# A mixture-of-experts stage on one Trainium2 core: routing scores in four column groups of TensorE, and two experts' weight splits moved to other places

## What is computed

```python
# layer 0, attention: even rows of each segment of 256 attend to each other, 16 heads of width 16, q = k = v
scores = jnp.einsum('bsqhd,bskhd->bshqk', qh, qh) * scale
attn = jax.nn.softmax(scores, axis=-1)
seg_out = jnp.einsum('bshqk,bskhd->bsqhd', attn, qh)
...
# layer 0, experts: E = 8, DIM = 256, FFN = 1024, x has 4096 rows
logits = x @ router_w + router_b
route = jax.nn.softmax(logits, axis=1)
max_prob = jnp.max(route, axis=1, keepdims=True)
max_ind = jnp.argmax(route, axis=1)
for e in range(num_experts):
    h = x @ w1[e]
    a, g = jnp.split(h, 2, axis=1)
    y = jax.nn.silu(a) * g @ w2[e]
    out = jnp.where((max_ind == e)[:, None], y, out)
out = out * max_prob
```

## Time and profile before

| quantity | value |
|---|---|
| runs, median (lowest, highest) | 1685.89 us (1683.33, 1692.66), 3 runs |
| the profiled execution, own time | 1684.51 us |
| its span, first to last instruction | 1682.8 us |
| mean granted TensorE clock | 0.937 of full speed |
| busy: PE, DVE, ACT, POOL | 1423.0, 941.7, 603.7, 668.2 us |

### The profile page before, as it was taken

One profiled execution on the slowest core, in us unless ns is written; L12 is line 12 of the kernel. 1 busy time (PEld: TensorE's weight loads), 2 busy tenths in 40 slices (PEclk: granted clock), 3 DMA queues, 4 the chain that ended last, 5 costly groups with the idle time before them and its releaser, 6 DMA issues. The chain is left out here.

```text
span 1682.8 us, 27329 instructions
## 1 busy us (share of the span) xinstructions
PE 1423.0 (85%) x8858; PEld 1216.5 (72%) x8859; DVE 941.7 (56%) x1802; ACT 603.7 (36%) x1015; POOL 668.2 (40%) x501
## 2 busy tenths in 40 slices
PE   6994546989989996499957999999999985999997
PEld 3442235878878885377756888888888874999997
DVE  4778441344444332377565776776776762555555
ACT  3443311222222332377532322322322322555553
POOL 6553344555555001511014555555555550531400
PEclk9996767999999998699978999999999997999999
DMA  4101332222120002600031253553543546554541
GB/s 147 54 25 58 118 127 76 84 86 93 68 100 19 16 13 76 206 1 1 1 100 51 63 140 110 150 137 112 150 134 115 150 132 230 188 191 167 192 143 44
DMA packets 109176, 171.15 MB, mean 102 GB/s; under 512 B 6112, under 2 KB 95072, under 8 KB 101696
## 3 DMA queue, kind: packets, MB, share of 16 engines
q1 hardware_dynamic: 100096, 156.00, 28.6%
q0 software_dynamic: 3408, 9.31, 1.9%
q10 hardware_dynamic: 5616, 5.11, 0.9%
HBM read 114.96 MB, written 55.44 MB: 101 GB/s over the span
## 5 line engine op out<-in xcount | busy, mean ns | idle before, releaser
L1448 PE MATMUL disp_psS<-disp_e,last_x 128*128 128x256 f32 x1024 | 240.4, 389 | 39.2 <-POOL disp_e L1538 20.5
L1448 PEld LDWEIGHTS disp_psS<-disp_e,last_x 128*128 128x128 f32 x1024 | 193.6, 194 | 70.9 <-POOL disp_e L1538 25.6
L1538 POOL TENSOR_TENSOR disp_e<-disp_e,disp_rs 128x1024 f32<-128x1024 f32 x64 | 152.4, 2380 | 119.9 <-DVE disp_rs L1567 119.9
L1567 DVE RECIPROCAL disp_rs<-disp_rs 128x256 f32<-128x256 f32 x64 | 112.2, 1753 | 135.4 <-POOL disp_rs L1536 135.4
L1498 ACT ACTIVATE disp_raw<-disp_psL 128x512 f32<-128x512 f32 x128 | 76.1, 595 | 290.2 <-DVE disp_top L1579 220.3
L1706 PE MATMUL comb_psO<-comb_yh,comb_eh 128*128 (+1 forms) x512 | 155.6, 304 | 14.1 <-DVE comb_el L1797 10.5
L1534 POOL TENSOR_TENSOR disp_s<-disp_e 128x512 f32<-128x512 f32 x64 | 81.6, 1275 | 203.5 <-ACT disp_e L1520 203.5
L1433 PE MATMUL disp_psL<-phi_hi,disp_xh 128*128 (+1 forms) x512 | 156.3, 305 | 5.4 <-DVE disp_e L1587 5.4
L1433 PE MATMUL disp_psL<-phi_lo,disp_xh 128*128 (+1 forms) x512 | 145.2, 284 | 0.0
L1433 PE MATMUL disp_psL<-phi_hi,disp_xl 128*128 (+1 forms) x512 | 145.0, 283 | 0.0
L1706 PE MATMUL comb_psO<-comb_yh,comb_el 128*128 (+1 forms) x512 | 144.7, 283 | 0.0
(11 more groups left out here) (256 smaller groups left out, 3537.6 us busy)
## 6 DMA issues: line engine op xcount, KB each, us to landing
logits<-disp_raw SPq DMA_DIRECT2D x64, 512.0 KB, 4.0
comb_e<-logits SPq DMA_DIRECT2D x32, 1024.0 KB, 4.9
w_raw<-in_w SPq DMA_DIRECT2D x8, 2048.0 KB
disp_wt<-in_w_slot SPq DMA_DIRECT2D x16, 1024.0 KB, 8.6
w_raw<-in_w SPq DMA_DIRECT2D x8, 1024.0 KB
disp_bt<-in_b_slot SPq DMA_DIRECT2D x8, 1024.0 KB, 11.3
slot_y<-disp_yb SPq DMA_DIRECT2D x64, 128.0 KB, 2.7
comb_y_in<-slot_y SPq DMA_DIRECT2D x4, 2048.0 KB, 10.3
```

The source lines that it names most:

```text
L1448: last = nc.tensor.matmul(psS[kd][:, b, :], x[:, b * TB + mc, kd * P:(kd + 1) * P], e[mc % 4][:, b, :], start=mc == 0 and b % 2 == 0, stop ...
L1538: nc.gpsimd.tensor_tensor(e[mc % 4][:], e[mc % 4][:], rs[mc % 2][:].unsqueeze(1).to_broadcast([P, B, BLK]), ALU.mult).then_inc(share_ready, 1)
L1567: v.reciprocal(rs[mc % 2][:], rs[mc % 2][:]).then_inc(rsum_ready, 1)
```

## The change

Four edits.

1. Router scores: the router's weights `rw` stand in 32 columns per chunk (`EW`), of which the last 24 are zero (POOL clears the buffer first, and SP's load waits for that). A group's four tiles are scored by eight products with 128 columns moving, tile `a` into output partitions 32a to 32a+31 of one 128x128 PSUM tile. ACT copies 128x128 in place of 8x512, and one transpose turns back four tiles' scores. DVE reads the 8 live columns of 32.
2. Expert 0's split leaves the routing block. ACT makes 1/16 of the high part per segment of the attention, after the copy of the next segment's rows (`high_slice`, 256 and 128 columns), and POOL 1/16 of the low part, two segments behind its masks (`low_slice`).
3. Expert 1's low part leaves the routing block: POOL makes it in the experts block, between the fourth and the fifth gather.
4. SP's load of expert 1 waits on `split` as before; the count is now reached by the attention's last slice.

```diff
--- before.py
+++ after.py
@@ -176,6 +176,7 @@
         out_raw, outT_ready, out_turned, rden_ready, heads_ready, fin, ones_set = (
             m.sem(s) for s in ("out_raw", "outT_ready", "out_turned", "rden_ready", "heads_ready", "fin", "ones_set"))
         even_loaded = [m.sem(f"even_loaded{i}") for i in range(2)]
+        w0_high = m.sem("w0_high")
         block = ctx.enter_context(nc.Block())
 
         def pair(i, k, lag):
@@ -235,11 +236,17 @@
                         xm[g][:], xT[q][:, half, :].unsqueeze(1).to_broadcast([P, UH, P]),
                         c["headmask"][:, part * UH:(part + 1) * UH].unsqueeze(2).to_broadcast([P, UH, P]),
                         ALU.mult).then_inc(xm_ready, 1)
+                    if g == UPS - 1:
+                        seg = i * 2 + q - 2
+                        if not isinstance(i, int) or seg >= 0:
+                            weights.low_slice(pool, seg, w0_high)
 
             fill_constants(nc, c, pool)
             masks(0)
             with pool.Fori(1, NSEG // 2) as i:
                 masks(i)
+            for seg in range(NSEG - 2, NSEG):
+                weights.low_slice(pool, seg, w0_high)
 
         @block.tensor
         def _(pe):
@@ -379,6 +386,9 @@
                 at = segment(i, k, -1)
                 if at is not None:
                     augment(*at, i + 1 + (k + 1) // 4)
+                at = segment(i, k, 3)
+                if at is not None:
+                    weights.high_slice(act, at[0], w0_high)
 
             keep_x(0, 0)
             act.wait_ge(ones_set, 4)
@@ -498,6 +508,7 @@
     m = Scope(nc, ctx, "route")
     XB = 3
     GT = 4
+    EW = P // GT
     with ctx:
         mean = m.sb("mean", [P, NT])
         rstd = m.sb("rstd", [P, NT])
@@ -505,8 +516,8 @@
         tmp = m.sb("tmp", [P, NT])
         magic = m.sb("magic", [P, NT], I32)
         xT = [m.sb(f"xT{i}", [P, KD, GT, P]) for i in range(2)]
-        logit_t = [m.sb(f"logit_t{i}", [NE, GT * P]) for i in range(2)]
-        rw = m.sb("rw", [P, KD, NE])
+        logit_t = [m.sb(f"logit_t{i}", [P, P]) for i in range(2)]
+        rw = m.sb("rw", [P, KD, EW])
         rb = m.sb("rb", [P, NE])
         logit = m.sb("logit", [P, NT, NE])
         best = m.sb("best", [P, NT])
@@ -530,11 +541,12 @@
         slots1 = m.sb("slots1", [P, NT, NCOL])
         ids = m.sb("ids", [P, NT, 2 * NCOL], BF16)
         psX = [m.ps(f"psX{i}", [P, 2, KD, P]) for i in range(XB)]
-        psL = [m.ps(f"psL{i}", [NE, GT * P]) for i in range(2)]
-        psR = m.ps("psR", [P, NT, NE])
+        psL = m.ps("psL", [P, P])
+        psR = m.ps("psR", [P, NT, EW])
         psAB = m.ps("psAB", [P, 2, NT, NE])
         psA, psB = psAB[:, 0], psAB[:, 1]
         psI = m.ps("psI", [P, 2 * NCOL])
+        rw_clear = m.sem("rw_clear")
         (w_loaded, chain, kept, turned, xT_ready, scored, scores_ready, routed, diff_ready, exp_ready,
          onehot_ready, counted, tables_ready, gathered, stored) = (m.sem(s) for s in (
              "w_loaded", "chain", "kept", "turned", "xT_ready", "scored", "scores_ready", "routed", "diff_ready",
@@ -543,7 +555,8 @@
 
         @block.sync
         def _(sp):
-            sp.dma_start(rw[:], router_w.rearrange("(k p) e -> p k e", p=P)).then_inc(w_loaded, 16)
+            sp.wait_ge(rw_clear, 1)
+            sp.dma_start(rw[:, :, 0:NE], router_w.rearrange("(k p) e -> p k e", p=P)).then_inc(w_loaded, 16)
             sp.dma_start(rb[:], router_b.partition_broadcast(P)).then_inc(w_loaded, 16)
             weights.load(sp, 1)
             for b in range(B):
@@ -554,8 +567,7 @@
 
         @block.gpsimd
         def _(pool):
-            weights.divide_low(pool, 0)
-            weights.divide_low(pool, 1)
+            nc.gpsimd.memset(rw[:], 0.0).then_inc(rw_clear, 1)
 
         @block.tensor
         def _(pe):
@@ -569,17 +581,17 @@
 
             def score(g):
                 wait(pe, xT_ready, g * 2 + 2)
-                wait(pe, scores_ready, g - 1)
+                wait(pe, scores_ready, g)
                 for k in range(KD):
-                    last = nc.tensor.matmul(psL[g % 2][:], rw[:, k, :], xT[g % 2][:, k].rearrange("p a t -> p (a t)"),
-                                            start=k == 0, stop=k == KD - 1)
+                    for a in range(GT):
+                        last = nc.tensor.matmul(psL[a * EW:(a + 1) * EW, :], rw[:, k, :], xT[g % 2][:, k, a, :],
+                                                start=k == 0, stop=k == KD - 1, skip_group_check=True)
                 last.then_inc(scored, 1)
 
             def turn_back(g):
                 wait(pe, scores_ready, g + 1)
-                for a in range(GT):
-                    last = nc.tensor.transpose(psR[:, g * GT + a, :], logit_t[g % 2][:, a * P:(a + 1) * P], c["ident"][0:NE, 0:NE])
-                last.then_inc(routed, 1)
+                nc.tensor.transpose(psR[:, g * GT:(g + 1) * GT, :].rearrange("p t e -> p (t e)"), logit_t[g % 2][:],
+                                    c["ident"][:]).then_inc(routed, 1)
 
             pe.wait_ge(w_loaded, 32)
 
@@ -605,12 +617,10 @@
 
         @block.scalar
         def _(act):
-            weights.divide_high(act, 0)
-
             def out(g):
                 act.wait_ge(scored, g + 1)
                 wait(act, routed, g - 1)
-                nc.scalar.activation(logit_t[g % 2][:], psL[g % 2][:], ACT.Copy).then_inc(scores_ready, 1)
+                nc.scalar.activation(logit_t[g % 2][:], psL[:], ACT.Copy).then_inc(scores_ready, 1)
 
             for i in range(NT // 2):
                 g = i // 2
@@ -642,7 +652,7 @@
                 v.tensor_scalar(x1[:, t, :], x1[:, t, :], mean[:, t:t + 1], rstd[:, t:t + 1], ALU.subtract, ALU.mult).then_inc(kept, 1)
             dve.wait_ge(w_loaded, 32)
             dve.wait_ge(routed, NT // GT)
-            link(v.tensor_tensor(logit[:], psR[:], rb[:].unsqueeze(1).to_broadcast([P, NT, NE]), ALU.add))
+            link(v.tensor_tensor(logit[:], psR[:, :, 0:NE], rb[:].unsqueeze(1).to_broadcast([P, NT, NE]), ALU.add))
 
             link(v.tensor_reduce(best[:], logit[:], X, ALU.max))
             bc = lambda ap: ap.unsqueeze(2).to_broadcast([P, NT, NE])
@@ -745,6 +755,24 @@
         sp.dma_start(self.raw1[:], self.w1_dram[e].rearrange("(k p) f -> p k f", p=P)).then_inc(self.loaded1, 16)
         sp.dma_start(self.raw2[:], self.w2_dram[e].rearrange("(k p) d -> p k d", p=P)).then_inc(self.loaded2, 16)
 
+    def high_slice(self, act, seg, ready):
+
+        for loaded, raw, hi, _ in self.parts():
+            act.wait_ge(loaded, 16)
+            n = KD * 2 * FF // NSEG if raw is self.raw1 else FK * D // NSEG
+            last = self.nc.scalar.activation(hi[:, 0, bass.ds(seg * n, n)], raw[:].rearrange("p k f -> p (k f)")[:, bass.ds(seg * n, n)], ACT.Copy)
+        last.then_inc(ready, 1)
+
+    def low_slice(self, pool, seg, ready):
+
+        pool.wait_ge(ready, seg + 1)
+        for _, raw, hi, lo in self.parts():
+            n = KD * 2 * FF // NSEG if raw is self.raw1 else FK * D // NSEG
+            last = self.nc.gpsimd.tensor_tensor(lo[:, 0, bass.ds(seg * n, n)], raw[:].rearrange("p k f -> p (k f)")[:, bass.ds(seg * n, n)],
+                                                hi[:, 0, bass.ds(seg * n, n)].bitcast(F32), ALU.subtract)
+        if isinstance(seg, int) and seg == NSEG - 1:
+            last.then_inc(self.split, 4)
+
     def parts(self):
         return ((self.loaded1, self.raw1, self.hi1, self.lo1), (self.loaded2, self.raw2, self.hi2, self.lo2))
 
@@ -757,7 +785,7 @@
     def divide_low(self, pool, e):
 
         for n, (_, raw, hi, lo) in enumerate(self.parts()):
-            pool.wait_ge(self.high, 2 * e + n + 1)
+            pool.wait_ge(self.high, 2 * (e - 1) + n + 1)
             self.nc.gpsimd.tensor_tensor(lo[:, e, :], raw[:].rearrange("p k f -> p (k f)"), hi[:, e, :].bitcast(F32),
                                          ALU.subtract).then_inc(self.split, 2)
 
@@ -836,6 +864,8 @@
                                              bass.IndirectOffsetOnAxis(route["token"][:, slot:slot + 1], 0)).then_inc(gathered[q], 16)
 
             for slot in range(SLOTS):
+                if slot == 4:
+                    w.divide_low(pool, 1)
                 gather(slot)
             nc.gpsimd.memset(w.zero[:], 0.0).then_inc(w.zeroed, 1)
             pool.wait_ge(w.zeroed, 1)
```

## The result

| group | kernel before, median (runs) | changed kernel, median (runs) | ratio, 95% interval |
|---|---|---|---|
| first pair | 1687.43 (4) | 1671.14 (4) | 0.9901 [0.9879, 0.9924] |
| 2 | 1650.56 (7) | 1617.82 (4) | 0.9819 [0.9781, 0.9857] |
| 3 | 1652.44 (7) | 1620.07 (4) | 0.9803 [0.9779, 0.9827] |
| 4 | 1653.81 (7) | 1618.61 (4) | 0.9798 [0.9764, 0.9833] |
| 5 | 1688.27 (9) | 1668.14 (2) | 0.9889 [0.9813, 0.9965] |

The forecast was 1649 and the range 1640 to 1664; the first pair gave 1671.14, so the change is faster, but by 16 us and not by 36. The kernel before has two levels, 1650 to 1654 in four of these groups and in group 1 (1650.00), and 1687 to 1688 in two, so kernels are compared only within a group.

The account below looks back on a forecast made before the run. The prediction had POOL's SBUF subtractions stalling DVE, and so PE, in routing, PE pacing the scores, and gathers delaying PE's reports in the experts: 1684.5 - 24.0 - 12.4 + 0.5 + 0 = 1648.6, forecast 1649, range 1640 to 1664.

Parts of the forecast that it names:

- Norm and scores: Routing: without POOL's subtraction and with narrow score products, DVE starts the logit sum at 165.4 instead of 189.44, saving 24.0 us.
- the extra 0.18: Scores on PE: two changes between full and narrow form per group, 0.09 us each, raising a group from 1.72 to 1.90.
- Counting: Routing: DVE's five additions take at most 2.3 us instead of 14.69, saving 12.4 us.
- Attention: Expert 0's split slices on ACT and POOL fit in gaps; cost taken 0.5 us for the block, bounds 0 and 18.
- Experts: Expert 1's low part between gathers makes the stream end 13.5 us later; cost taken 0, bounds -20 and +13.5.
- the hold: Experts: what PE reports reaches other engines late during POOL's gathers, at worst until 3.9 us behind the last.
- The rival with the longer hold: Experts: PE's reports stay late longer because the gather stream ends 13.5 us later; 1662.5 us, chance 0.12.
- a late report of PE: During a stream of POOL's gathers, what PE reports reaches the others late, at worst only when the stream is over.
- the forecast of that wait's end: Experts: ACT's longest wait should end 4 us behind the last gather, near 70 us from the first.
- The case "nobody is held": Experts: the gathers delay no engine, as the reason for the delay isn't known; 1629 us, chance 0.06.

Follow-up runs that it names:

- one gather more in front: Changed kernel with expert 1's low part behind five gathers instead of four: 1618.11 us, against 1617.82 for the changed kernel.
- the kernel with nine late gathers: Changed kernel with expert 1's low part behind five gathers and the last nine gathers behind expert 2's split: 1616.00 us; 1647.34 in group 5.
- Groups 4 and 5: Changed kernel with expert 1's low part back in the routing block: 1626.28 against 1618.61 us, then 1671.24 against 1668.14.
- The twelve pieces: Changed kernel with expert 1's low part as twelve instructions of 512 columns, still between the fourth and fifth gather: 1614.36 us, one run.
- the six pieces: Changed kernel with expert 1's low part in six pieces of 1024 columns, one behind every six gathers: 1629.44 us.
- the four gathers: Changed kernel with only the first four gathers, every slot's rows read from those four tiles in turn: 1622.02 us, one run.
- group 6: Changed kernel with ten gathers, expert 1's low part behind the fifth, then expert 2's split, then the other 29 gathers: 1638.28 us, against 1619.68 for the changed kernel.

## Why the prediction was wrong

- **Norm and scores** (24.0 saved): right, 23.0 by the rows (189.44 to 166.40). A group was to take 1.90 and took 1.70. The sum without the extra 0.18 was 1.72, and the 0.18 was counted twice: each change of form costs the 0.09 that was read in the attention, but the 1.02 and the 0.57 went from the start of one form to the start of the next and already held one such step each. In the narrow view of PE (the last transpose, the turning back, the first of the narrow products) two starts of one form are 0.11 apart, and the start of the new form is 0.21 behind the last of the old:

```profile
156.47 0.27 PE L579 MATMUL route_psX<-const_ident,first_x 128*128 128x128 f32 x1
156.58 0.27 PE L593 MATMUL route_psR<-const_ident,route_logit_t 128*128 128x128 f32 x1
156.79 0.32 PE L587 MATMUL route_psL<-route_xT,route_rw 128*32 128x128 f32 x4
```

The Trainium skill (TensorEngine Tiling (Array Packing), Tiling Modes, Key Properties) states that a change of the tiling mode drains TensorE; the 0.1 us more agrees with it. What six groups gave so, 1.1 us, was less than the 1.9 by which the first scores ended later than forecast (153.86, not 152.0); 1.55 of that is a later start of the norm (148.39 against 146.84), which is no cost of the change: two profiles of each kernel show both values (146.6 to 146.8, and 148.4).
- **Counting** (12.4 saved): right, 12.42 (14.69 to 2.27).
- **Attention** (0.5): POOL's slices took 1.14 where 1.13 was said and lay in its gap; masks still start every 7.6 to 7.7 us.
- **Experts** (0 taken, 17.8 lost): here it failed. The failed step is the sentence that the first 13.5 us "are now free of gathers, and PE gets one to two slots further before it is held". It gets no further. One result is out before the hold, as before: the first comes at 39.4 behind the first gather (33.1 in group 5), the second at 68.8 (69.0), and so 12.5 later than before, as the stream ends 12.1 later (64.5 against 52.4). In the meantime PE even falls back: it starts the last of the third slot's first products (L897) at 41.9 behind the first gather, and in the kernel before (L867) at 32.4.
- **What took the quiet time**: in part POOL's low part, which holds DVE's copy of the second slot's rows for 13.66 us, and PE waits 5.44 for it. The prediction had read this same lock in routing and priced it in the attention, and left it out where the 13.45 us had been moved to. In group 2, without the stretch, the lock costs 4.7 at the first result and one gather more in front takes that away (26.6). With the stretch it is argued, not shown by itself: the kernel with nine late gathers, whose copy is free, is a slot further (second result at 43.2, stream to 53.5; the kernel before 56.3, stream to 52.4), but the changed kernel with only the fifth gather moved wasn't run in a group with the stretch. The other 8 of the 13 us at the first result (39.4 against 31.2 in group 2) came with the stretch, with idle times of PE and ACT behind 220 put down to "issue" and "remote".
- First the row, then the rule: the copy stood for 13.66 us beside two POOL instructions of 13.40 together. The Trainium skill (SBUF — State Buffer, SBUF: two separate sides) states that a GpSimd instruction and a DVE one in a two-port mode or with two SBUF inputs shut each other out for a whole instruction; the trace agrees, and goes further, with 15.05 us behind twelve short ones.
- The rival with the longer hold, 1662.5, had the size of this (13.5; the lead fell by 12.5 to the second result), but I gave it 0.12, on the ground that PE had four slots' worth of quiet, where its own text on the experts has one to two. From the second to the last result another 5.3 us went; the first 4 of it are a gap of 13.3 between the second and third result. Groups 4 and 5 put the move's price in the experts at 11.2 with the slow stretch and at 3.3 without by the medians (7.7 left of some 11), 5.5 by the two profiles of group 4 (last result at 418.1 against 412.6). The other 6.6 of the 17.8 aren't explained: two profiles of the changed kernel with the stretch differ by 4.5 there (450.2 and 445.7).
- **Behind the experts** (nothing taken): 2.2 us between the last result and the linear attention's first gather, and 3.0 in its slow stretch (67.7 to 70.7 from its first gather to the first `phi_lo`). The 2.2 is in fifteen of the eighteen traces of kernels with the changed code, where POOL's idle time in front of that gather (134.05 after) is put down to "issue"; before it is 131.71 put down to POOL's queue. The twelve pieces, the six pieces and the four gathers of group 1 don't have it (3.3 us from last result to gather, as before, and not 5.4 to 5.7). What POOL does in it the profile doesn't show. The 3.0 varied from group to group (69.0 in group 5 for the changed kernel).
- 0.45 at the first gather, 17.8 in the experts, 2.2, 3.0 and 0.3 behind them make 23.8 of the 24.0 us between the forecast's 1648.6 and 1672.59.
- **What the slow stretch is**: I read a late report of PE. ACT's start 20.7 us behind PE's product bears that out, but PE was also starting its own products late, which I hadn't seen. The time of its end, 3.9 us behind the last gather, was right, and the forecast of that wait's end, "near 70 us from the first", was too (68.5). Only who is through by then was wrong.

In a group without the stretch the change brings 32 to 35 us, near the 36 of the forecast. That is in part luck: the experts' 3.3 to 5.5 and the 2.2 behind them were in no term there either. The case "nobody is held" gave 1629 and not the 1618 measured, since it took off 20 us for the experts' stream and left in the 17 that the linear attention's stream costs.

**Open.** What makes the stretch appear: two of seven groups of runs have it, in all kernels of the group. The chip of group 5 has the same number as that of group 3, which was quiet, so the number doesn't decide it. Nine gathers over slots inside the loop don't bring it on; whether 29 would, group 6 couldn't say, as it was quiet. The linear attention's stream of 32 does.

## What to carry to other kernels

When a long POOL instruction is moved, list what DVE does at its new place as you did at the old one: the lock moves with it, and even a copy of 0.28 us waits for all of it. Cutting the instruction up didn't help where the pieces followed each other at once (15.05 us); with six gathers between the pieces the copies were held 2.3 at most, though the last piece then came too late for PE, and placing the whole behind the copy that it would catch left that copy at 0.28. Then look at what POOL's queue is late for: of the versions here the best has five gathers, the low part, 25 gathers, the next split and the last nine gathers: 4.1, 2.6 and 20.8 us under the changed kernel in three groups, the first two of them no more than the spread of one kernel's runs (3 to 6 us).

## What the hardware showed

- The same kernel can have, in some groups of runs, a stretch in which PE, ACT and DVE all start late while POOL issues a stream of indirect DMAs: products up to 2.8 us apart instead of 0.23, an ACT copy 20.7 us behind the product it needs, until 2.7 to 4.2 us past the last gather. Over the two streams of the kernel before it costs 19.8 us (last result at 432.4 against 412.6) and 16.8 (first `phi_lo` at 67.7 against 50.9), together about the step from 1650 to 1687. A stream of nine in such a group cost nothing.
- A DVE copy that waits beside two or twelve of POOL's low-part instructions isn't let in between them: 13.66 and 15.05 us, though its record starts 0.09 and 0.11 us before POOL's. In other places an instruction of DVE does get in: in the count's additions the first took 8.68 us, the length of POOL's first instruction, and the copy of 259.84 in group 2 ended at 266.13, just as POOL's high part (258.96 + 7.01) did, with the low part following at 266.06.
- Four column groups with 32 columns each did eight products in 0.57 us (156.79 to 157.36) in fp32, adding two chunks into the same outputs, where two products with 8 columns by 512 took 1.82. Where PE goes between that form and 128x128, the next start comes 0.1 us later than within one form.
